# Where four engines' side work stands inside a scan of 64 tiles: softplus sums one by one, lower weight parts apart from du, the router in two groups

## The reference

```python
u = silu(conv(in_proj(ctx)))                       # 4 batches, 256 channels, 256 steps
dt_lo, Bm, Cm = split(x_proj(u))                   # 8, 16, 16 rows
delta = softplus(dt_proj(dt_lo) + dt_proj_b)
def step(state, xs):                               # over the 256 steps, per channel e and state n (16)
    d_t, B_t, C_t, u_t = xs
    dA = exp(d_t[..., None] * A)
    state = state * dA + (d_t * u_t)[..., None] * B_t[:, None, :]
    y_t = einsum('ben,bn->be', state, C_t)
    return (state, y_t)
x = x + tanh(g_xattn) * (y + D * u) * silu(layernorm(x))
logits = layernorm(x) @ gate_w                     # 8 experts, top 2, softmax of the two
x = x + tanh(g_ffn) * sum_of_two(cw * (silu(h @ w0) * (h @ w1)) @ wo)   # h = layernorm(x)
```

## Time and profile before

| What | us |
|---|---|
| median of 3 runs | 307.88 |
| lowest and highest | 307.65, 309.58 |
| the profiled execution | 307.61 |
| its span, first to last instruction | 305.8 |
| DVE busy in the whole span | 229.0 |
| PE busy in the whole span | 265.8 |

### The profile page before, as it was taken

The page is one execution under the profiler, slowest core; times in us unless marked ns, Lnnn a source line. Parts: engine busy times, 40 slices in busy tenths (PEclk is TensorE's granted clock), DMA queues, the critical chain, the costliest instruction groups (busy, mean ns, idle before and its releaser), DMA issues.

```text
span 305.8 us, 4685 instructions
## 1 busy us (share of the span) xinstructions
PE 265.8 (87%) x1166; PEld 178.1 (58%) x1167; DVE 229.0 (75%) x398; ACT 188.4 (62%) x349; POOL 183.2 (60%) x162
## 2 busy tenths in 40 slices
PE   8984698789788999897889489999999999999970
PEld 8432243234234345363565357988889898888960
DVE  2839999997889999999899664656565665656640
ACT  1894577865765685768484844565665657566540
POOL 5000449996999898998590442355547465565442
PEclk9996979999999999999999778999999999999996
DMA  7699200000000000001059611123242332423222
GB/s 233 225 395 387 94 2 0 0 1 0 0 0 3 1 0 0 0 2 69 1 184 331 242 49 39 29 41 57 48 69 40 63 51 52 68 35 69 28 26 34
DMA packets 16659, 22.70 MB, mean 74 GB/s; under 512 B 2554, under 2 KB 10274, under 8 KB 16642
## 3 DMA queue, kind: packets, MB, share of 16 engines
q1 hardware_dynamic: 11456, 16.41, 15.2%
q0 software_dynamic: 4416, 6.03, 11.9%
q10 hardware_dynamic: 770, 0.06, 0.2%
HBM read 17.38 MB, written 5.11 MB: 74 GB/s over the span
## 4 chain that ended last, share of the span: by engine, by line
PE 54%; DVE 23%; issue 11%; ACT 6%; POOL 3%; POOLq 1%; DVEq 0%; ACTq 0%
PE PD L1025 11%; PE PZ L1061 11%; PE PU L1025 10%; PE PY L844 7%; DVE states L1216 6%; DVE states L1222 5%; PE PY L1047 3%; DVE u L1142 2%; POOL hC L411 2%; PE PZ L1016 2%; PE PU L823 1%; PE PU L830 1%; PE PU L752 1%; ACT PD L612 1%; DVE WO L1240 1%
## 5 line engine op out<-in xcount | busy, mean ns | idle before, releaser
L411 POOL TENSOR_TENSOR hC<-states,WO 128x512 f32<-128x512 f32 x63 | 79.5, 1272 | 19.6 <-DVE states L1222 9.2
L1222 DVE TENSOR_TENSOR_SCAN states<-PD,states 128x512 f32<-128x512 f32 x64 | 77.3, 1209 | 1.3 <-ACT PD L612 1.0
L844 PE MATMUL PY<-hC,ident 128*128 128x512 f32 x128 | 68.9, 623 | 7.2 <-POOL hC L411 6.9
L446 POOL DMA_INDIRECT out<-lg,y_at x23 | 36.4, 1581 | 49.3 <-ACT lg L718 41.9
L612 ACT ACTIVATE PD<-WO,Aneg 128x510 f32<-128x510 f32 x64 | 43.9, 688 | 18.2 <-DVE states L1222 15.5
L1216 DVE TENSOR_TENSOR states<-PU,WO 128x512 f32<-128x512 f32 x64 | 42.7, 668 | 2.7 <-POOL hC L411 1.6
L402 POOL TENSOR_TENSOR W_lo<-W,W_hi 128x512 fp32r<-128x512 f32 x25 | 32.5, 1308 | 11.5 <-ACT W_hi L523 11.5
L1459 DVE TENSOR_TENSOR dA<-PU,dA 128x512 f32<-128x512 f32 x23 | 15.9, 691 | 28.5 <-PE PU L1025 28.5
L702 ACT ACTIVATE hidT_hi<-PY 128x512 fp32r<-128x512 f32 x23 | 13.8, 598 | 38.0 <-PE PY L1047 38.0
L1471 DVE TENSOR_TENSOR WO_lo<-WO,WO_hi 128x512 fp32r<-128x512 f32 x46 | 29.7, 688 | 9.4 <-issue 9.3
L844 PEld LDWEIGHTS PY<-hC,ident 128*128 128x128 f32 x128 | 21.9, 191 | 23.4 <-POOL hC L411 17.3
(11 more groups left out here) (245 smaller groups left out, 507.2 us busy)
## 6 DMA issues: line engine op xcount, KB each, us to landing
W<-in_L_ffn_w SPq DMA_DIRECT2D x16, 512.0 KB, 10.9
WO<-in_L_ffn_wo SPq DMA_DIRECT2D x8, 512.0 KB, 8.4
xs<-in_x SPq DMA_DIRECT2D x2, 512.0 KB, 5.5
out<-xs SPq DMA_DIRECT2D x2, 512.0 KB, 3.2
x_rows<-u SPq DMA_DIRECT2D x2, 512.0 KB, 5.9
early<-in_ctx SPq DMA_DIRECT2D x1, 512.0 KB, 4.2
hC<-x_rows,x_at POOLq DMA_INDIRECT x23
out<-lg,y_at POOLq DMA_INDIRECT x23, 3.8
```

Source lines behind the costliest of these rows:

```text
L411: pool.tensor_tensor(hC[:, n % 2, :], states[:, n % RING, :], C_rep[:, pair % C_RING, :], ALU.mult).then_inc(hc_done, 1)
L446: pool.indirect_dma_start(out=out, out_offset=bass.IndirectOffsetOnAxis(ap=y_at[:, s:s + 1], axis=0), in_=y_tile[s % 2], in_offset=None, c ...
L844: pe.matmul(PY[:, h, :], ident[:, :], hC[:, n % 2, :], start=False, stop=(m == DS - 1)).then_inc(y_done, 1)
L1222: dve.tensor_tensor_scan(states[:, n % RING, :], DEC[n % 2], states[:, n % RING, :], 0.0, ALU.mult, ALU.add).then_inc(scan_done, 1)
```

## The change

The same instructions stand in other places of the queues, and two functions are cut in pieces so that their pieces can be placed singly: `delta_sum` in its three terms, `router` in its two halves.

```diff
-SUM_AT, DELTA_AT, DU_AT = (14, 17), (20, 23), (22, 25)
-TURN_X_AT, X_OUT_AT, BASE_AT, BASE_OUT_AT = (24, 36), (29, 41), (30, 42), (35, 47)
-ADD_X_AT, ADD_GZ_AT, X2_OUT_AT = (48, 49), (50, 51), (55, 56)
-ADD_NEXT_AT = 59
-ROUTER_AT, LOGITS_AT, STATS_AT = 57, 60, (56, 57, 59)
+SUM_AT, DELTA_AT, DU_AT = ((11, 13, 15), (17, 18, 19)), (20, 24), (22, 29)
+TURN_X_AT, X_OUT_AT, BASE_AT, BASE_OUT_AT = (25, 37), (30, 42), (31, 43), (36, 48)
+ADD_X_AT, ADD_GZ_AT, X2_OUT_AT = (49, 50), (51, 52), (56, 57)
+ADD_NEXT_AT = 60
+ROUTER_AT, LOGITS_AT, STATS_AT = (58, 59), 62, (57, 58, 60)
...
-SPLIT_AT = tuple(range(4, 58, 3))
+SPLIT_AT = (3, 6, 9, 12, 15, 18, 24, 26, 31, 33, 36, 39, 41, 44, 47, 49, 52, 54)
...
-            def delta_sum(c):
+            def delta_sum(c, part):
...
-                pe.matmul(DRAW[c], ident[:, :], sp_relu[c], start=True, stop=False)
-                pe.matmul(DRAW[c], neg_id[:, :], sp_rest[c], start=False, stop=False)
-                pe.wait_ge(sp_ln_ok, c + 1)
-                pe.matmul(DRAW[c], ident[:, :], sp_ln[c], start=False, stop=True).then_inc(delta_ps, 1)
+                if part == 0:
+                    pe.matmul(DRAW[c], ident[:, :], sp_relu[c], start=True, stop=False)
+                elif part == 1:
+                    pe.matmul(DRAW[c], neg_id[:, :], sp_rest[c], start=False, stop=False)
+                else:
+                    pe.wait_ge(sp_ln_ok, c + 1)
+                    pe.matmul(DRAW[c], ident[:, :], sp_ln[c], start=False, stop=True).then_inc(delta_ps, 1)
...
-            def router(q):
+            def router(q, h):
...
-            delta_sum(2)
-            through(SUM_AT[0] + 1, SUM_AT[1] + 1)
-            delta_sum(3)
-            through(SUM_AT[1] + 1, TURN_X_AT[0] + 1)
+            at = RAW_AT
+            for c in (2, 3):
+                for part in range(3):
+                    through(at, SUM_AT[c - 2][part] + 1)
+                    delta_sum(c, part)
+                    at = SUM_AT[c - 2][part] + 1
+            through(at, TURN_X_AT[0] + 1)
...
-            through(at, ROUTER_AT + 1)
-            router(0)
-            at = ROUTER_AT + 1
+            for h in range(2):
+                through(at, ROUTER_AT[h] + 1)
+                router(0, h)
+                at = ROUTER_AT[h] + 1
```

More of the change, by code:

```diff
@@ L902, in add_gz @@
                 mm.then_inc(x2_ps, 1)
-            def router(q):
+            def router(q, h):
                 pe.wait_ge(gc_ok, 3)
[L907 to L915, removed]
+                pe.wait_ge(gz_ok, 2 * q + h + 1)
+                if not q:
+                    pe.wait_ge(x2_ok, QB)
+                for r in range(QBLK):
+                    at = h * 64 + r * E
+                    mm = pe.matmul(LOGITS[q][h][:, at:at + E], z_cols[:, q * QBLK + 2 * (r // 2) + h, r % 2, :],
+                                   gc_gz[:, h, :], start=True, stop=True)
+                mm.then_inc(logit_ps, 1)
             def ranks():
@@ L941, in _ @@
             delta_raw(3)
-            through(RAW_AT, SUM_AT[0] + 1)
-            delta_sum(2)
-            through(SUM_AT[0] + 1, SUM_AT[1] + 1)
-            delta_sum(3)
-            through(SUM_AT[1] + 1, TURN_X_AT[0] + 1)
+            at = RAW_AT
[5 more added lines that the diff above has]
+            through(at, TURN_X_AT[0] + 1)
             turn_x(0)
@@ L981, in _ @@
             pe.wait_ge(W_hi_ok, 1)
-            router(1)
+            router(1, 0)
+            router(1, 1)
             for r in range(QB):
```

## The result

| | us |
|---|---|
| kernel before, median (lowest, highest) | 307.98 (307.65, 309.58) |
| changed kernel, median (lowest, highest) | 312.21 (311.12, 313.09) |
| ratio, 95% interval | 1.0123 (1.0082 to 1.0164) |
| span of the profiled execution, before and after | 305.8, 310.6 |

The change makes the kernel 4.2 us slower. Forecast were 305.8 us and a range up to 307.5, so the prediction was wrong, and in its sign. In the profiled executions the loss is 4.8 us of span. Both profiles begin the scan at the same time, so their times compare directly.

What follows compares the result with a forecast made beforehand. VectorE was taken to bound the scan, so only its waits could be saved: 3.9 us removed, 0.4 + 0.55 + 0.8 + 0.2 = 1.95 back in, gain 1.95, forecast 305.8 us; eight in ten within 304.2 to 307.5.

Steps and rivals of the forecast that it cites:

- Removed: Stalls of VectorE at tiles 19 to 29, from softplus sums and POOL's lower parts: 3.9 us to be taken away.
- delta_out(3) at tile 24: Late after the last softplus sum, its chain ending just as scan(24) wants it: cost zero to 0.4, taken as 0.
- Back in at drive(31) and drive(33): What stays of the 2.0 us of POOL stalls after moving lower parts from du: 0.4, bounds 0 and 1.0.
- Early: SPLIT_AT starting at 3, not 4, delays hC(4) and drive(8) by 0.7: net cost 0.55, bounds 0.3 and 0.8.
- POOL's reserve: How late POOL's hC may start after its scan without delaying a drive: 1.8 us, at 1.24 per product.
- Tiles 36 to 57: Eight lower parts instead of seven, and a later chain at tiles 56 and 57: net cost 0.8, bounds 0 and 1.5.
- the walk: Going through each queue in order at the durations of the earlier trace to find which starts come late.
- Logits: Router behind spread_C(31), which waits for drive(61): VectorE waits 1.6 instead of 1.3, cost 0.2, bounds -0.3 and 0.6.
- After the scan: Behind the last scan only one add_x changes place and all else shifts: no term in the sum.
- The port rival: VectorE's lower part beside POOL's after the scan: 1.1 us goes or comes again, 304.7 or 306.9, chance 0.05.

Runs made afterwards that it cites:

- e6: Kernel before with only the six softplus sums placed one at a time, after tiles 11, 13, 15, 17, 18, 19: 306.42 us, ratio 0.9896.
- e3: Changed kernel with the router's first half after tile 57 and its second after 58: 309.39 us, ratio 1.0018.
- e7: Kernel before with only the change's SPLIT_AT, DU_AT and DELTA_AT (POOL's lower parts and du, delta_out): 309.41 us, ratio 1.0006.
- e1: Changed kernel with both router halves back after tile 57, logits still after scan(61): 305.98 us, ratio 0.9912.
- e4: Changed kernel plus five unread PE products after tile 57, filling the idle time ahead of spread_C(31); router still after 58 and 59: 305.79 us, ratio 0.9909.
- e5: Changed kernel with router and logits as before (both halves after tile 57, logits after scan(59)): 309.20 us, ratio 0.9995.
- e8: Changed kernel with both router halves after tile 57, logits after scan(61), and two unread PE products behind the router: 305.71 us, ratio 0.9873.
- e9: Kernel before plus three unread PE products behind the router's groups of tile 57: 308.51 us, ratio 0.9978.
- e10: Kernel before plus unread PE products in the routing only, four ahead of low_part(3) and two after the first block's turn: 308.84 us, ratio 0.9982.
- e11: e8 with the first SPLIT_AT entries put back to 4, 7, 10, 13, 16: 305.74 us, ratio 0.9868.
- e12: e11 plus the unread PE products in the routing of e10: 304.32 us, ratio 0.9817.
- e2: Kernel before with only the router part of the change: halves after 58 and 59, logits after scan(61), second add_x after 60: 309.40 us, ratio 1.0026.

## Why the prediction was wrong

Its steps one by one, by the table of stalls above.

- **Removed, 3.9 us**: right. The stalls at tiles 20 to 29 were 3.94 and are nothing in the changed kernel. The split into 1.8 of PE's sums and 2.0 of POOL's lower parts is too neat: e6 alone takes 1.13 of the 2.05 as well, so PE's lump had pushed POOL behind; each part alone leaves something, both together nothing.
- **delta_out(3) at tile 24, taken as 0**: right, 0 in the changed kernel, 0.84 if it stays at tile 23.
- **Back in at drive(31) and drive(33), 0.4**: right, 0.36.
- **Early, 0.55, bounds 0.3 and 0.8, "the surest of the terms"**: outside its bounds, 1.27 less 0.16 = 1.11. drive(8) lost its 0.7, but the lower parts after 6 and 9 cost another 0.5 at scan(9) and drive(14), which I had left to POOL's reserve. The reserve was counted with 1.24 per product, from the x2 of the earlier trace rows; the x3 of the same rows takes 3.90, 1.30 each. That this is the reason is not shown. The 0.75 at tile 7 of the table is also not always there: five profiled executions with this SPLIT_AT whose scan(0) is at 30.05 us or later have it, the two with 29.7 (e3, e7) do not.
- **Tiles 36 to 57, 0.8**: right, 0.42 + 0.79 less 0.35 = 0.86, with ScalarE's PD awaited at 56 and 57 as said.
- **Up to scan(58)** this makes 1.60, where the walk has 3.9 - 0.4 - 0.55 - 0.8 = 2.15. The difference is the early term.
- **The variance**: no step had it. It took 1.12 in place of 0.34, and the gap between two scans in which it stands grew by 0.77 (1.43 against 0.66 over 1.71). It took 1.12 in e1, e4, e5 and e8 as well, so it is not the clock's.
- **Logits, 0.2, bounds -0.3 and 0.6**: the step that failed. Its order is right: both halves stand behind spread_C(31), and e4 shows the wait of this queue, 1.36, under the 1.6 that I walked. But "four blocks of router T + 2.2 to 3.1 (half of the 1.94 of the earlier trace rows)" prices PE at the clock of before, while the same paragraph moves the router away from the only idle time that it had filled. I saw that spread_C(31) waits for drive(61), and did not ask what PE does meanwhile: 2.28 us of nothing. At a clock of 0.50 the wait is 3.85, which costs 2.5 more than before in place of 0.2.
- **After the scan, "nothing is reordered apart from the place of one add_x, and all shifts"**: wrong for the same reason. The sums of the last tiles at half the clock make hC(63) wait 1.75, and that shifts it beside POOL's lower parts: from scan(63) to MAX8 2.45 us are lost. The 0.60 behind MAX8 lie within what executions differ there.
- **The port rival** (1.1 either way) came in both forms at once: hC(63) is 0.82 longer beside POOL, the lower part at 162.00 is 1.09 shorter.

None of the rivals had the clock; a time over 311 was given 0.03, as "more than these queues could cost". As to queues that holds: without the fallen clock the same order takes 305.79 (e4), 0.1 from the forecast's 305.9. That nearness is luck. The walk lacked 0.77 for the variance and 0.56 of the early term, and before itself was 308.71 in that batch. Nor is the gain of e4 one number: by the ratio of the medians, 0.9909, it is 2.8 us, but the median of before holds executions with a low clock; between the two profiled executions, both at 1.00 through the scan, scan(63) comes 0.94 earlier and the end 0.85. The forecast 1.95 lies between the two.

What stays open: why the mean clock is 0.950 or less in seven of ten executions of e5 and in 23 of 63 of before, with the same hole of 1.37 us; what decides the clock's course in the routing; and how much of e9's gain is real.

## What to carry to other kernels

When a change moves work of PE out of an idle stretch, write down the hole that it leaves and the granted clock of the rows around it, and price everything behind the hole at both levels; a queue walk at the old durations is only one of the two cases. Here side work of PE was worth most where PE would have idled waiting for VectorE, and unread products in such a hole are a cheap test of whether the clock is the cause. Read the clock in the stretch that matters: the mean of an execution does not say where it fell. Moves inside a long scan can be forecast to a few tenths by walking each queue, if the walk goes past the first stall to the second and third; here it did not, and the early term came out at 1.11 for 0.55.

## What the runs showed of the hardware

- **PE's clock falls behind short holes, and not in every execution.** Nine profiled executions (before, after and seven experiments) had a hole of 0.52 to 2.28 us ahead of spread_C(31); in seven of them the clock is 0.50 behind it, for about 3 to 10 us; in before and e10, with holes of 1.37 and 1.38, it stays at 1.00. Of the five with the hole filled (e4, e8, e9, e11, e12) none shows a fall there. e1, with a hole of only 0.52:

```profile
147.00:150.00 3.00, 3.00 (x5) 1.12 (x4) 2.90 (x7) 1.96 (x4) 1.35 (x2) 0.50 0.00 0
```

- **A small DVE instruction waits out one of POOL.** The variance is a TENSOR_SCALAR on 128x4 elements. In the changed kernel it runs from 144.59 to 145.71; POOL's row there is

```profile
143.09 2.59 POOL L411 TENSOR_TENSOR hC<-states,WO 128x512 f32<-128x512 f32 x2 [0.70 <-PE PY L844]
```

  whose second hC ends at 145.68. Before, it ran from 144.48 to 144.82, and the second of POOL's three hC starts at 143.53 and ends at 144.80. Both end with POOL's instruction, within 0.03, and so do those of e1, e4, e5 and e8, which take 1.12 too. In e7 POOL is idle from 142.66 to 143.08; there the variance starts at 142.87 and takes 0.17. The Trainium skill, page "SBUF — State Buffer", section "Who interferes with whom", says that a tensor_scalar can enter a mode of two ports in which it and GpSimd shut each other out for a whole instruction; these rows agree. By them the price is not the 0.17 of the operation but whatever is left of POOL's 1.3, and it moves by 0.8 when two queues shift by as little.
- **Two operands in SBUF**: hC(63) of 128x512 took 1.52 where POOL's lower parts were under way (from 156.60) when it started at 158.11. It took 0.70 before, where it started at 154.78, 0.11 ahead of the first of them. In e2, e3 and e5, where it starts behind the first lower part, it took 1.15, 0.85 and 1.40.
- **A clock of 0.50 through the routing** goes with 27.6 to 27.7 us from MAX8 to the first expert, in seven profiled executions, against 26.1 to 26.9 in the other seven. That the clock is the cause is not shown.
